# Three of four second layer chunks of a mixture FFN as fp32r hi/lo products, with both parts of the GELU output made on VectorE

## What is computed

```python
rw = softmax(x.mean(axis=1) @ Wr + br)                 # per batch
tk_w, tk_i = top_k(rw_tok, 2);  tk_w = softmax(tk_w)
h = gelu(einsum('nd,edf->enf', x_flat, W1) + b1[:, None, :])
expert_out = einsum('enf,efd->end', h, W2) + b2[:, None, :]
out = einsum('ne,end->nd', cw, expert_out)             # cw: the two weights of a token
y = layernorm(out + x) * gamma + beta                  # and this is added to the input
```

## Time and profile before

| what | us |
|---|---|
| median of 3 runs (683.65 to 685.68) | 685.32 |
| the profiled execution, as timed | 685.26 |
| its span, first to last instruction | 683.5 |
| PE busy in the span | 619.5 |
| ACT busy | 487.8 |
| DVE busy | 457.5 |
| POOL busy | 358.2 |

### The profile page before, as it was taken

One profiled execution on the slowest core, in us unless ns is written; L12 is line 12 of the kernel. 1 busy time (PEld: TensorE's weight loads), 2 busy tenths in 40 slices (PEclk: granted clock), 3 DMA queues, 4 the chain that ended last, 5 costly groups with the idle time before them and its releaser, 6 DMA issues.

```text
span 683.5 us, 20582 instructions
## 1 busy us (share of the span) xinstructions
PE 619.5 (91%) x5067; PEld 497.2 (73%) x5067; DVE 457.5 (67%) x1439; ACT 487.8 (71%) x1101; POOL 358.2 (52%) x538
## 2 busy tenths in 40 slices
PE   4899999999999999999949617999999999999882
PEld 3677777777777777777737415999999999998872
DVE  3999998989898989898939661333333333333696
ACT  3788888888888888888838513665666666665585
POOL 5778888888888888888846630000000000000585
PEclk9999999999999999999989756999999999999997
DMA  3010221012101211021271102322232322321033
GB/s 109 25 32 10 63 58 57 15 54 61 54 29 40 61 54 43 26 61 38 64 227 33 37 27 73 96 85 85 80 87 80 87 81 84 85 82 42 31 109 108
DMA packets 85339, 44.02 MB, mean 64 GB/s; under 512 B 7737, under 2 KB 84289, under 8 KB 85313
## 3 DMA queue, kind: packets, MB, share of 16 engines
q1 hardware_dynamic: 85312, 43.70, 22.0%
HBM read 30.83 MB, written 12.85 MB: 64 GB/s over the span
## 4 chain that ended last, share of the span: by engine, by line
PE 83%; DVE 7%; issue 3%; SPq 2%; ACT 2%; DMA 1%; POOL 0%; DVEq 0%; POOLq 0%; ACTq 0%
PE banks L475 17%; PE bank L344 16%; PE bank L356 8%; PE banks L369 6%; PE bank L382 5%; PE bank L341 5%; PE bank L465 5%; PE bank L467 5%; PE bank L466 5%; PE bank L330 3%; PE bank L322 2%; PE bank L318 2%; PE bank L392 2%; DVE ln_stats L904 2%; PE bank L317 2%
## 5 line engine op out<-in xcount | busy, mean ns | idle before, releaser
L649 ACT ACTIVATE q_by_row_group<-bank,b_all 128x256 f32<-128x256 f32 x268 | 126.9, 474 | 95.5 <-PE bank L467 95.5
L893 DVE SCALAR_TENSOR_TENSOR yT<-banks,slot_weight,yT x268 | 73.0, 284 | 145.6 <-PE banks L475 139.7
L1042 POOL TENSOR_TENSOR probs<-probs,row_sum_recip 128x512 f32<-128x512 f32 x128 | 133.5, 1043 | 65.8 <-DVE row_sum_recip L780 63.8
L475 PE MATMUL banks<-q_by_row_group,w_all 128*128 128x256 f32 x536 | 159.6, 380 | 0.0
L344 PE MATMUL bank<-k_by_head,q_by_row_group 128*128 128x256 f32 x512 | 132.9, 383 | 0.0
L465 PE MATMUL bank<-gathered,w_hi 128*128 (+1 forms) x268 | 126.5, 472 | 4.5 <-DMA gathered<-z_split 4.5
L1088 POOL TENSOR_TENSOR w_lo<-w_all,w_hi 128x512 fp32r<-128x512 f32 x8 | 10.2, 1274 | 190.7 <-ACT w_hi L629 190.7
L344 PEld LDWEIGHTS bank<-k_by_head,q_by_row_group 128*128 128x128 f32 x512 | 99.3, 194 | 14.3
L764 DVE TENSOR_REDUCE row_max<-bank 128x8 f32<-128x512 f32 x128 | 88.0, 687 | 29.7 <-PE bank L344 29.6
L591 ACT ACTIVATE probsT<-bank 128x512 f32<-128x512 f32 x128 | 76.4, 597 | 28.0 <-PE bank L356 26.3
L767 DVE TENSOR_REDUCE row_sum<-probs 128x8 f32<-128x512 f32 x128 | 86.8, 678 | 10.7 <-ACT probs L582 10.2
(11 more groups left out here) (148 smaller groups left out, 1013.8 us busy)
## 6 DMA issues: line engine op xcount, KB each, us to landing
gathered<-z_split SPq DMA_DIRECT2D x272, 64.0 KB, 1.8
z_split<-z_hi_lo SPq DMA_DIRECT2D x32, 256.0 KB, 2.6
x_res<-in_x SPq DMA_DIRECT2D x16, 256.0 KB, 2.9
ctxT_pair<-in_ctxT SPq DMA_DIRECT2D x32, 128.0 KB, 2.1
w_all<-in_w SPq DMA_DIRECT2D x16, 256.0 KB, 4.5
out<-k_by_head SPq DMA_DIRECT2D x16, 256.0 KB, 2.3
z_split<-yT SPq DMA_DIRECT2D x2, 128.0 KB, 2.5
wq<-in_wq SPq DMA_DIRECT2D x1, 64.0 KB, 2.5
```

The costliest lines, as they stand in the source:

```text
L475: nc.tensor.matmul(ps, W2F[:, e, c, :], G[:, c, :], start=(c == 0), stop=(c == FC - 1)).then_inc(p_c, 1)
L649: nc.scalar.activation(G[:, c, :], bank[c][:, 0:BT], ACT.Gelu, bias=B1A[:, e, c:c + 1]).then_inc(a_g, 1)
L1042: nc.gpsimd.tensor_tensor(pp, pp, RC[:, k % 2, :].unsqueeze(2).to_broadcast([128, 8, S]), ALU.mult).then_inc(g_norm, 1)
```

## The change

The first three chunks of the second layer (`SPLIT = 3`) become fp32r hi/lo products; the fourth stays one fp32 product.

- PE: `output` does three fp32r products for c < 3, from `W2H`, `W2L` (weights) and `GH`, `GL` (GELU). It waits for the lo part of the chunk (`v_gl`) in place of the GELU's semaphore.
- DVE: `split_gelu(g, c)` waits for the GELU and for PE's reading of the chunk before it, copies `G` to `GH` (rounding to fp32r), waits for that copy, and subtracts into `GL`. In the loop the three splits of block g + 1 come ahead of the combines of block g; the first block's splits stand before the loop, the last block's combines behind it.
- ACT: the GELU of a chunk c < 3 waits for `v_gl` in place of `p_c`. Per expert it also makes `W2H`, 128x384; the wait for the second weights moves here from PE.
- POOL: per expert also `W2L`, 128x384, and it starts when both hi parts are made.

```diff
+SPLIT = 3
+        W2H = sb("w2_hi", [128, 2, SPLIT, D], F32R)
+        W2L = sb("w2_lo", [128, 2, SPLIT, D], F32R)
+        GH = sb("gelu_hi", [128, SPLIT, BT], F32R)
+        GL = sb("gelu_lo", [128, SPLIT, BT], F32R)
...
                 if c == 0:
                     pe.wait_ge(v_c, GB * g + GB)
-                pe.wait_ge(a_g, 4 * g + (4 + c + 1))
-                nc.tensor.matmul(ps, W2F[:, e, c, :], G[:, c, :], start=(c == 0), stop=(c == FC - 1)).then_inc(p_c, 1)
+                if c < SPLIT:
+                    pe.wait_ge(v_gl, SPLIT * g + (SPLIT + c + 1))
+                    nc.tensor.matmul(ps, W2H[:, e % 2, c, :], GH[:, c, :], start=(c == 0), stop=False)
+                    nc.tensor.matmul(ps, W2H[:, e % 2, c, :], GL[:, c, :], start=False, stop=False)
+                    nc.tensor.matmul(ps, W2L[:, e % 2, c, :], GH[:, c, :], start=False, stop=False).then_inc(p_c, 1)
+                else:
+                    pe.wait_ge(a_g, 4 * g + (4 + c + 1))
+                    nc.tensor.matmul(ps, W2F[:, e, c, :], G[:, c, :], start=False, stop=True).then_inc(p_c, 1)
...
-            pe.wait_ge(g_wlo, 1)
-            pe.wait_ge(d_w2, 16 * E)
+            pe.wait_ge(g_wlo, 2)
...
                 nc.scalar.activation(W1H[:, e % 3, :], W1R[:, e, :], ACT.Copy).then_inc(a_whi, 1)
+                act.wait_ge(d_w2, 16 * E)
+                nc.scalar.activation(W2H[:, e % 2, :, :], W2F[:, e, 0:SPLIT, :], ACT.Copy).then_inc(a_whi, 1)
...
                 act.wait_ge(p_h, 4 * g + (16 + c + 1))
-                act.wait_ge(p_c, 4 * g + (c + 1))
+                if c < SPLIT:
+                    act.wait_ge(v_gl, SPLIT * g + (c + 1))
+                else:
+                    act.wait_ge(p_c, 4 * g + (c + 1))
...
+            dve.nop().then_inc(v_gl, SPLIT)
+
+            def split_gelu(g, c):
+
+                dve.wait_ge(a_g, 4 * g + (4 + c + 1))
+                dve.wait_ge(p_c, 4 * g + (c + 1))
+                nc.vector.tensor_copy(GH[:, c, :], G[:, c, :]).then_inc(v_gh, 1)
+                dve.wait_ge(v_gh, SPLIT * g + (c + 1))
+                nc.vector.tensor_tensor(GL[:, c, :], G[:, c, :], GH[:, c, :], ALU.subtract).then_inc(v_gl, 1)
...
-            with dve.Fori(0, blocks) as g:
+            for c in range(SPLIT):
+                split_gelu(0, c)
+            with dve.Fori(0, blocks - 1) as g:
+                for c in range(SPLIT):
+                    split_gelu(g + 1, c)
                 combine(g)
+            combine(blocks - 1)
...
-                pool.wait_ge(a_whi, e + 1)
+                pool.wait_ge(a_whi, 2 * e + 2)
                 nc.gpsimd.tensor_tensor(W1L[:, e % 3, :], W1R[:, e, :], W1H[:, e % 3, :],
                                         ALU.subtract).then_inc(g_wlo, 1)
+                nc.gpsimd.tensor_tensor(W2L[:, e % 2, :, :], W2F[:, e, 0:SPLIT, :], W2H[:, e % 2, :, :],
+                                        ALU.subtract).then_inc(g_wlo, 1)
```

More of the change, by code:

```diff
@@ L197, in build @@
         p_h, a_g, p_c, v_c = sem("p_hidden"), sem("a_gelu"), sem("p_ffn_chunk"), sem("v_combined")
+        v_gh, v_gl = sem("v_gelu_hi"), sem("v_gelu_lo")
         d_w1, d_w2 = sem("d_w1_all"), sem("d_w2_all")
@@ L495, in _ @@
                 if e + 1 < E:
-                    pe.wait_ge(g_wlo, e + 2)
+                    pe.wait_ge(g_wlo, 2 * (e + 2))
                     both(end - 1, e, e + 1)
@@ L1085, in split_lo @@
             def split_lo(e):
-                pool.wait_ge(a_whi, e + 1)
+                pool.wait_ge(a_whi, 2 * e + 2)
                 nc.gpsimd.tensor_tensor(W1L[:, e % 3, :], W1R[:, e, :], W1H[:, e % 3, :],
                                         ALU.subtract).then_inc(g_wlo, 1)
-            split_lo(0)
-            for e in range(1, E):
+                nc.gpsimd.tensor_tensor(W2L[:, e % 2, :, :], W2F[:, e, 0:SPLIT, :], W2H[:, e % 2, :, :],
+                                        ALU.subtract).then_inc(g_wlo, 1)
+            for e in range(E):
                 split_lo(e)
```

## The result

The changed kernel takes 746.72 us (median of 4 runs, 743.84 to 748.46) against 684.49 us for the kernel before, run beside it (4 runs, 683.54 to 685.68): a ratio of 1.0904, 95% interval 1.0862 to 1.0946. It is slower by some 62 us. The profiled execution took 747.52 us, its span is 745.8 us; before the span was 683.5 us.

A forecast was written before the change was run, and what follows sets the result against it. DVE was to bound the expert stage with a 4.23 us turn in place of PE's 3.15: 66 turns make 71 us, plus 6 for POOL and 1 for the ends, 78 us on 685, so 763 us (range 722 to 805).

The forecast's parts named there:

- PE alone: Expert stage: three fp32r products replace an fp32 one in three chunks, 3.15 to 2.91 us a block, 16 us less.
- The copy: DVE's rounding of 128x256 to fp32r, once in each of three pairs a block: 0.336 us; the pairs together 1.79 us.
- The queue's part: DVE's turn outside the pairs: 2.19 us for loads, waits and combines in series, plus 0.25 us ahead of the first copy.
- turns of 3.27 and 5.2 us: Ends for DVE's turn: 3.27 us if queue work hides behind the engine, 5.2 us with slower copies and queue costs per pair.
- POOL and DVE: POOL's weight subtracts, 16 us over seven later experts, get in DVE's way: cost between 0 and 16 us, taken as 6.
- rival (c): POOL blocks DVE for all of its time, 16 us in place of 6: 773 us; chance 0.09.
- Routing: Routing chain at the start: another step stalls beside POOL in place of today's 1.28 us one; -1.1 to +1.2 us, taken as 0.
- The first block: Start of the expert stage: first block and last combine, paid once each, 1 us together.
- PE's stall: PE stands 1.3 us of each block at the first product whose subtract on DVE is late.
- (a): Rival: DVE's queue runs ahead of the engine, turn 3.27 to 3.7 us, total 699 to 728 us; chance 0.12.
- (b): Rival: faster, DVE's turn stays under PE's 2.91 us; full price -16 us, 669 us; chance 0.05.
- (d): Rival: PE's clock falls to 1.2 GHz, 5.3 us a block; 798 us with half of the blocks, 834 with all; chance 0.07.

The follow-up runs named there:

- e1: Against the changed kernel: PE keeps its three hi/lo products, ACT writes the hi part, the low part stays zero, DVE only combines; 669.96 us.
- e2: Against the changed kernel: all splitting work and waits stay, but PE multiplies all four chunks as fp32 products; 746.31 us.
- e5: Changed kernel without DVE's load of batch numbers and the addresses made from them; combines add to fixed columns (output of other batches); 700.50 us.
- e6: Changed kernel with nothing left out, the load of batch numbers moved between the second copy and its subtract; 722.95 us.
- e10: Changed kernel with the first expert's hi and lo weights used throughout, so weights are cut once (wrong weights in the output); 740.38 us.
- e4: Changed kernel with one chunk split (chunk 0) in place of three; 691.68 us, ratio 1.0092 to 1.0149 to the kernel before.
- e8: As e4, one chunk split, but the second chunk (c = 1) in place of the first; 679.75 us, ratio 0.9936 to the kernel before.
- e3: Changed kernel with two chunks split in place of three; 707.99 us, ratio 1.0312 to 1.0384 to the kernel before.

## Why the prediction was right, and where its sizes were off

The sign, the bound and its mechanism came as forecast: 746.7 us where 763 was predicted and 722 to 805 was the range. The forecast was 16 us too high, with its terms off in both directions. Point by point:

- **PE alone.** Predicted 2.91 us a block and 16 us for the stage; e1 shows 2.93 and 14.3. That none of it is kept in the change is shown by e2.
- **The copy** is the term of the sum that was mis-sized. It was taken as 0.336 us, from the line between two TENSOR_SCALAR rows; it takes 0.29. The page of the Trainium skill that was weighed against it (VectorE: DVE Perf Modes, The perf-mode tier table, with the fixed part of its section on the TRN2 errata) had led to an estimate of 0.29 us, and the trace agrees. With the subtract at 0.42 to 0.43 us and its follower 0.34 us behind, both as in the earlier trace rows, the pairs took 1.66 in place of 1.79 us, 66 x 0.13 = 9 of the 16 us by which the forecast was too high. The 395 ns row of 336 columns, on which I leaned, isn't explained by this.
- **The queue's part** was 2.19 + 0.25 = 2.44 us and measured 0.95 + 1.42 = 2.37; in total 66 x 0.07 = 5 us too high. The price of two turns in a row at the end of the kernel before was the right place to read it. That it stands in series was a choice between turns of 3.27 and 5.2 us; e5 and e6 show that it does. That the wait inside each pair is the reason, as the prediction has it, is argued: no run takes this wait out.
- **POOL and DVE.** Predicted 6 us between 0 and 16; e10 gives 6.3, with ACT's part in it. The turns at the changes of expert show 3.4 of it in the trace (five are some 0.53 us longer than the others, one 0.80), and most of the rest falls on the first block. DVE's timeline of the kernel after at a change of expert, then POOL's:

```profile
467.01 1.07 DVE L919 SCALAR_TENSOR_TENSOR yT<-banks,slot_weight,yT  x4 [0.53 <-issue]
468.42 0.82 DVE L906 CAST gelu_hi<-q_by_row_group 128x256 fp32r<-128x256 f32 x1 [0.34 <-ACT q_by_row_group L665]
```

```profile
466.84 1.29 POOL L1119 TENSOR_TENSOR w_lo<-w_all,w_hi 128x512 fp32r<-128x512 f32 x1 [42.31 <-ACT w_hi L642]
468.09 1.00 POOL L1121 TENSOR_TENSOR w_lo<-w_all,w_hi 128x384 fp32r<-128x384 f32 x1
```

  The copy that began beside POOL's subtract lasted till shortly after its end, 0.53 us longer than others. The POOL subtract of 128x384 takes 1.00 us, as estimated. The full 16 us of rival (c) weren't paid, since most of POOL's time fell on the queue and on combines, as the prediction argued. That the sum came out near 6 is in part luck: in e5, where the same two subtracts fall on a copy and a subtract of DVE, the changes cost 13.5 us. The Trainium skill (Advanced Engine Details and Errata, VectorE Performance Modes) states that GpSimd instructions and Vector instructions that use both ports block each other; the trace agrees for the copies.
- **Routing.** Another step (L864) stalls in the place of the old one, for 1.16 us in place of 1.28, so taking it as 0 held.
- **The first block** was part of 1 us; the first group of combines came 2.0 us late. Ahead of it the weights of the second expert are cut beside a pair of DVE, whose copy took 1.01 us and whose subtract 1.10. Without that cutting, in e10, the group came at 424.57 us, as early as before:

```profile
422.66 1.01 DVE L906 CAST gelu_hi<-q_by_row_group 128x256 fp32r<-128x256 f32 x1 [1.49 <-ACT q_by_row_group L665]
423.71 1.10 DVE L908 TENSOR_TENSOR gelu_lo<-q_by_row_group,gelu_hi 128x256 fp32r<-128x256 f32 x1
```

- **The sum of the misses.** The copy is 8.6 us too high, the queue's part 4.6 and the changes of expert 2.6 (3.4 for 6); the first block is 1.0 us too low. Together that is 14.8 of the 15.5 us by which the profiled run (747.52) stayed below 763.
- **PE's stall** was to be 1.3 us a block: it is 1.1 (4.03 - 2.93). Of the rivals, (a) is refuted by e5 and e6, (b) by the turn, and (d) by the clock of 1.00 with PE busy 17 of 20 us; (c) by its size in this kernel.

One gap in the working did no harm: it summed DVE's ring alone. PE's own queue, which cost e4 its gain, had no term; here PE's ring has room for it, since the GELU of chunk 0 is done 0.96 us before DVE takes it up. In e5, where DVE's turn is shorter, it sets the turn.

## What to carry to other kernels

Work moved to an engine off the path is priced by that engine's whole turn, and the turn includes what its queue does (loads of registers, branches, waits). Look for a place where two turns follow each other with nothing to wait for; that distance is the better price (2.37 us measured here for the 2.44 worked out from it, where the four combines alone are 1.07). If each step waits for the engine's own result, expect the queue in series; here it was. Work that blocks another engine is priced by where it falls in that engine's turn. Before a smaller version is given up, move it: put the split where the next engine's queue has little to do behind the wait, and put register loads beside an instruction that is waited for anyway.

## What the runs showed of the hardware beside this

- PE's queue isn't free behind a wait. After a stall at the split of chunk 0 the next product was late by "issue" (0.24 us, 55 times), and in e4, with PE full, products there took 0.17 and 0.14 us in place of 0.12. Behind chunk 1 they didn't (e8). At chunk 0 the next piece of the program, `hidden`, begins a new block and waits for its gathered input; the trace of the kernel after shows these waits as register instructions of PE's queue between the low half and the next weight load. No run leaves them out alone.
- A POOL subtract beside it stretches DVE's fp32 to fp32r copy of 128x256 from 0.29 to as much as 1.10 us, and DVE's subtract of 128x256 from 0.43 to as much as 1.10 us, till shortly after the end of POOL's instruction; how far the two overlap decides the size. The four combines, which read PSUM, took 1.07 us beside the same POOL subtract, as without it.
- Fewer splits don't mean less loss at the changes of expert. By the turns in the traces, six changes cost 3.4 us with three chunks (after), 8.2 with two (e3) and 8.5 with one (e4).
